# A graph layer and an expert layer on one core: who does the last blocks' work at the ends of the edge stages, and in which pieces the first dense batch runs

## The reference

```python
xn = layernorm(h, ln1);  q, k, v = xn@wq+bq, xn@wk+bk, xn@wv+bv       # per layer
scores = einsum('ehd,ehd->eh', q[dst], k[src]) / sqrt(32)            # edges and self loops
ex  = exp(scores - segment_max(scores, dst)[dst])
agg = segment_sum(ex/segment_sum(ex, dst)[dst] * v[src], dst)        # where deg > 0
h = h + agg@wo + bo
h = h + gelu(layernorm(h, ln2)@w1 + b1)@w2 + b2
...
x = x + h
out = x + layernorm(xf + sum of the two chosen experts' FFN(xf)),  xf = layernorm(x)
```

## Time and profile before

| what | value |
|---|---|
| median of 3 runs | 3311.08 us (3309.96 to 3312.67) |
| the profiled execution's own time | 3308.49 us |
| its span, first to last instruction | 3306.30 us |
| mean granted TensorE clock | 0.772 of full speed |
| busy: PE / DVE / ACT / POOL | 68% / 75% / 40% / 55% |
| DMA | 623.51 MB, mean 189 GB/s |

### The profile page before, as it was taken

One profiled execution on the slowest core, in us unless ns is written; L12 is line 12 of the kernel. 1 busy time (PEld: TensorE's weight loads), 2 busy tenths in 40 slices (PEclk: granted clock), 3 DMA queues, 4 the chain that ended last, 5 costly groups with the idle time before them and its releaser, 6 DMA issues. The chain is left out here.

```text
span 3306.3 us, 28610 instructions
## 1 busy us (share of the span) xinstructions
PE 2235.3 (68%) x7207; PEld 1510.9 (46%) x7207; DVE 2490.4 (75%) x3966; ACT 1320.9 (40%) x3886; POOL 1834.8 (55%) x1938
## 2 busy tenths in 40 slices
PE   6745666656566666699956665666666666699798
PEld 4423443433343343476643333344433433477676
DVE  6788888888888888545448888888888888455233
ACT  2224444445545444211224444554544544222222
POOL 5047777777777776212047777777777775221000
PEclk8866767677777766799976777777677767699899
DMA  5357777777777778323357777777777777332111
GB/s 145 105 169 236 243 243 243 243 243 243 245 246 246 243 243 244 84 62 86 82 162 236 244 243 243 243 245 245 246 246 243 244 243 234 78 79 55 45 32 39
DMA packets 249750, 623.51 MB, mean 189 GB/s; under 512 B 50258, under 2 KB 105777, under 8 KB 249592
## 3 DMA queue, kind: packets, MB, share of 16 engines
q0 software_dynamic: 149904, 471.38, 47.9%
q1 hardware_dynamic: 99688, 150.30, 14.6%
HBM read 526.66 MB, written 94.78 MB: 188 GB/s over the span
## 5 line engine op out<-in xcount | busy, mean ns | idle before, releaser
L811 POOL DMA_INDIRECT ring<-kv_table,stage_ix x1760 | 1672.7, 950 | 601.6 <-issue 539.7
L1078 PE MATMUL bank<-ring,hot_w 128*128 128x272 f32 x1760 | 709.9, 543 | 516.9 <-DVE ring L2026 467.3
L1065 PE MATMUL bank<-qs,hot_q 128*128 x1760 | 691.5, 535 | 358.4 <-DVE ring L2003 295.6
L1078 PEld LDWEIGHTS bank<-ring,hot_w 128*128 128x128 f32 x1760 | 418.1, 259 | 790.9 <-DVE ring L2026 630.6
L2003 DVE TENSOR_TENSOR ring<-ring,bank 128x1024 f32<-128x1024 f32 x440 | 533.7, 1213 | 282.0 <-DMA ring<-kv_table,stage_ix 254.9
L1065 PEld LDWEIGHTS bank<-qs,hot_q 128*128 128x128 f32 x1760 | 444.6, 263 | 513.0 <-issue 423.9
L2008 DVE TENSOR_REDUCE s<-ring 128x32 f32<-128x1024 f32 x440 | 533.9, 1213 | 4.2
L1293 ACT ACTIVATE hot_q<-pos_b,row_of 128x128 f32<-128x128 bf16 x880 | 301.0, 392 | 25.2 <-DVEq L1991 16.5
L2020 DVE TENSOR_TENSOR bank<-ring,bank 128x512 f32<-128x512 f32 x440 | 301.8, 686 | 0.0
L2017 DVE TENSOR_TENSOR ring<-ring,bank 128x512 f32<-128x512 f32 x440 | 297.7, 677 | 0.0
L2026 DVE TENSOR_TENSOR ring<-ring,bank 128x512 f32<-128x512 f32 x440 | 295.9, 673 | 0.4
(11 more groups left out here) (333 smaller groups left out, 2214.8 us busy)
## 6 DMA issues: line engine op xcount, KB each, us to landing
agg_d<-stage_o SPq DMA_DIRECT2D x108, 544.0 KB, 4.4
ring<-kv_table,stage_ix POOLq DMA_INDIRECT x1760, 3.8
pos_b<-rel_d SPq DMA_DIRECT2D x54, 256.0 KB, 5.4
kv_table<-ring SPq DMA_DIRECT2D x50, 224.0 KB
h_dram<-ring SPq DMA_DIRECT2D x15, 560.0 KB
ring<-h_dram SPq DMA_DIRECT2D x15, 560.0 KB
ring<-in_x_dram SPq DMA_DIRECT2D x10, 560.0 KB
ring<-kv_table SPq DMA_DIRECT2D x10, 560.0 KB
```

The source lines that it names most:

```text
L811: gps.indirect_dma_start(out=chunk[:, par * G + i, j, :], out_offset=None, in_=table, in_offset=bass.IndirectOffsetOnAxis(ap=stage_ix[:, p ...
L1065: mm = ten.matmul(q_bank(third, i)[:, 0:QC], hot_q[:, i % 4, a * P:(a + 1) * P], qs[:, bass.ds(t * QC + a * QC, QC)], start=(a == 0), stop ...
L1078: mm = ten.matmul(b_acc[i % 2][:, lo - OWN:MC], hot_w[:, i % 4, :], chunk[:, s, j, lo:ROW], start=(j == 0), stop=(j == QD // 2 - 1), skip_ ...
```

## The change

It has six parts.

1. For the last blocks of each layer, `weigh_late` multiplies all four rows of a block in one VectorE instruction, and the second pair of rows is added to the first by GpSimd (`add_pairs`), behind all its gathers. These are blocks 2 to 7 of the last full group and all four of the last group. VectorE's order in the last two steps is written anew: in the last full group two late multiplications stand ahead of the last score product.
2. SP waits until the last block's gathers have landed before it issues the weight loads.
3. PE's `fold` is cut into `fold_rows` and `fold_ups`. The row part for mid, and the up part for last, are issued inside the links, ahead of the sums over first rows; the up part for mid stays behind the links.
4. The first batch's home gathers count a semaphore per tile (`first0` to `first4`), and VectorE's `first_head` works tile by tile: denominators, own term and division of a tile, mixed with the addition of the projected tile and statistics of earlier ones. The bias is added at the start.
5. PE projects tile j - 1 of that batch right behind the transposes of tile j.
6. `hold` becomes a plain wait wherever its counter was read by nobody.

```diff
+LATE = 2
+assert LASTG == LATE + 2 and LATE + 3 == G - 3
+HEAD0 = 5 * BT + 1
...
                     if nn == LASTG:
+                        sp.wait_ge(gath[(NB - 1) % SLOTS], (layer + 1) * uses((NB - 1) % SLOTS) * QD * 16)
                         next_weights()
                     if nn:
...
-                                               in_offset=bass.IndirectOffsetOnAxis(ap=stage_h[:, j:j + 1], axis=0)).then_inc(s["home"], 16)
+                                               in_offset=bass.IndirectOffsetOnAxis(ap=stage_h[:, j:j + 1], axis=0)).then_inc(s["home"] if it else S[f"first{j}"], 16)
...
-                            hold(pool, S["agg"], (k - 2) * G + (layer * NB + i + 1), S["pool_passed"])
+                            pool.wait_ge(S["agg"], (k - 2) * G + (layer * NB + i + 1))
...
+                def add_pairs(par, i, n):
+
+                    pool.wait_ge(S["weighed"], n + 1)
+                    val = chunk[:, par * G + i, :, D:ROW]
+                    gps.tensor_tensor(val[:, 0:2], val[:, 0:2], val[:, 2:4], ALU.add).then_inc(S["w_ready"], 1)
+
                 for k in range(NGRP):
                     group(k, k % 2, blocks_of(k), k < 2)
+                for k in range(NGRP - 2, NGRP):
+                    for i in range(LATE if k == NGRP - 2 else 0, blocks_of(k)):
+                        add_pairs(k % 2, i, layer * NB + k * G + i)
 
...
-            def fold(kind):
+            def fold_rows(kind):
 
                 pe.wait_ge(S["w_in_dma"], 16 * W_TOTAL[kind])
-                mm = None
                 if kind in ("in", "mid"):
                     for c0, c1, b in ((0, 512, bank[7 if kind == "in" else 4]), (512, 768, bank[2 if kind == "in" else 5])):
                         for a in range(2):
                             mm = ten.matmul(b[0:TN, 0:c1 - c0], g_col[:, 1, a:a + 1].to_broadcast([P, TN]), w_qkv[:, a, c0:c1], start=(a == 0), stop=(a == 1))
-                if kind in ("mid", "last"):
-                    for f in range(FFN // P):
-                        for a in range(2):
-                            mm = ten.matmul(bank[6][:, f:f + 1], w_up[:, a, f * P:(f + 1) * P], g_col[:, 3, a:a + 1], start=(a == 0), stop=(a == 1))
+                    mm.then_inc(S["w_pe"], 1)
+
+            def fold_ups(kind):
+
+                pe.wait_ge(S["w_in_dma"], 16 * W_TOTAL[kind])
+                for f in range(FFN // P):
+                    for a in range(2):
+                        mm = ten.matmul(bank[6][:, f:f + 1], w_up[:, a, f * P:(f + 1) * P], g_col[:, 3, a:a + 1], start=(a == 0), stop=(a == 1))
                 mm.then_inc(S["w_pe"], 1)
 
...
-                turn(0)
-                project(0, 0)
+                for j in range(BT + 1):
+                    if j < BT:
+                        turn_tile(0, j)
+                    if j:
+                        project_tile(0, 0, j - 1)
...
                 mm.then_inc(S["l_pe"], 1)
+                if layer:
+                    fold_ups("last")
+                else:
+                    fold_rows("mid")
                 pe.wait_ge(S["l_dve"], layer * L_DVE + L_FIRST)
                 for a in range(2):
...
             links(0)
-            fold("mid")
+            fold_ups("mid")
             pe.wait_ge(S["w_dve"], 2)
...
             links(1)
-            fold("last")
             pe.wait_ge(S["w_dve"], 3)
             staggered("last")
...
-                v.wait_ge(S["w_pe"], PASS_NO[kind] + 1)
+                v.wait_ge(S["w_pe"], {"in": 1, "mid": 2, "last": 4}[kind])
...
                 if kind in ("mid", "last"):
+                    v.wait_ge(S["w_pe"], {"mid": 3, "last": 4}[kind])
                     ws.did(tt(up_bias[:, :], up_bias[:, :], bank[6][:, 0:FFN // P], ALU.add))
                     for a in range(2):
...
+                def first_head(h, st):
+
+                    hd = Steps(s["head"])
+                    v.wait_ge(s["x_in"], 2 * ROWS)
+                    hd.did(bias(h_n[kind], bias_sq))
+                    v.wait_ge(s["out_free"], 1)
+
+                    def put(j):
+                        v.wait_ge(s["mm"], j + 1)
+                        tt(h[:, j, :], h_n[kind][:, j, :], bank[4 + j % 3][0:TN, 0:D], ALU.add).then_inc(s["bank_free"], 1)
+
+                    def stats(j):
+                        v.wait_ge(s["bank_free"], j + 4)
+                        st.did(vec.bn_stats(stat[:, j, :], h[:, j, :]))
+
+                    for j in range(BT):
+                        v.wait_ge(S[f"first{j}"], (1 if kind == "mid" else 2) * 16)
+                        own, z = home[:, j, 0:H], home[:, j, H:2 * H]
+                        val = home[:, j, 2 * H:MC].rearrange("p (d h) -> p d h", h=H)
+                        den = small[0:TN, j * H:(j + 1) * H]
+                        mine = own_v[:, j, :].rearrange("p (d h) -> p d h", h=H)
+                        hd.did(tt(den, z, own, ALU.add))
+                        hd.did(tt(mine, mine, own.rearrange("p (a h) -> p a h", a=1).to_broadcast([TN, DH, H]), ALU.mult)); hd.sync(v)
+                        hd.did(ts(den, den, 1e-30, None, ALU.max))
+                        hd.did(tt(mine, mine, val, ALU.add)); hd.sync(v)
+                        hd.did(vec.reciprocal(den, den)); hd.sync(v)
+                        tt(tok[:, j, :].rearrange("p (h d) -> p d h", h=H), mine, den.rearrange("p (a h) -> p a h", a=1).to_broadcast([TN, DH, H]), ALU.mult).then_inc(s["tok"], 1)
+                        if j >= 2:
+                            put(j - 2)
+                            if j >= 3:
+                                stats(j - 3)
+                    assert hd.n == HEAD0, hd.n
+                    put(BT - 2)
+                    stats(BT - 3)
+                    put(BT - 1)
+                    stats(BT - 2)
+                    stats(BT - 1)
+                    st.sync(v)
+                    aggregate()
+
...
-                head(0)
                 st = Steps(s["dve"])
-                projected(0, 0, 0, h_of[0], st)
+                first_head(h_of[0], st)
                 rooted(0)
...
+                def weigh_late(par, i, n):
+
+                    val = chunk[:, par * G + i, :, D:ROW].rearrange("p j (d h) -> p j d h", h=H)
+                    w = w_of[:, i].rearrange("p j (a h) -> p j a h", a=1)
+                    tt(val, val, w.to_broadcast([P, QD, DH, H]), ALU.mult).then_inc(S["weighed"], 1)
+
...
                     ch.did(vec.tensor_reduce(top[:, 0:nk * H].rearrange("p (b h) -> p b h", h=H), s, AX.X, ALU.max))
-                    if not first:
+                    if not nn:
+                        weigh_late(1 - par, G - 3, n - 3)
+                    elif not first:
                         weigh(1 - par, G - 3, n - 3)
                     ch.sync(v)
                     ch.did(tt(s[:, :, :, QD], s[:, :, :, QD], pen[:, :, QD:QD + 1].to_broadcast([P, nk, H]), ALU.add))
-                    if not first:
+                    if not nn:
+                        weigh_late(1 - par, G - 2, n - 2)
+                    elif not first:
                         halve(1 - par, G - 3, n - 3)
                         weigh(1 - par, G - 2, n - 2)
                     v.wait_ge(S["lanes"], (k + g0) * 2 + 1)
@@ -2048,11 +2126,13 @@
                     ch.did(vec.tensor_tensor_scan(f_lane[lanes, :], pen_now[lanes, 0:P], b_ch[lanes, 0:P], -BIG, ALU.add, ALU.max))
                     ch.sync(v)
                     ch.did(vec.tensor_tensor_scan(m_lane[lanes, ::-1], pen_now[lanes, 1:P + 1][:, ::-1], f_lane[lanes, ::-1], -BIG, ALU.add, ALU.max))
-                    if not first:
+                    if nn and not first:
                         halve(1 - par, G - 2, n - 2)
                     if nn:
                         scores(1 - par, 0, tn, n + nk, third + 1)
-                    if not first:
+                    if not nn:
+                        weigh_late(1 - par, G - 1, n - 1)
+                    elif not first:
                         weigh(1 - par, G - 1, n - 1)
                     if nn:
                         sum_scores(1 - par, 0, n + nk)
@@ -2060,15 +2140,38 @@
                     m = b_ch[:, P:P + nk * H].rearrange("p (b h a) -> p b h a", h=H, a=1).to_broadcast([P, nk, H, QD + 1])
                     ch.did(tt(s, s, m, ALU.subtract))
                     assert ch.n == CHAIN
-                    if not first:
+                    if nn and not first:
                         halve(1 - par, G - 1, n - 1)
+
+                    def sum_weights():
+                        v.wait_ge(S["weights"], (k + g0) * 2 + 2)
+                        vec.tensor_reduce(chunk[:, par * G:par * G + nk, 0, WOFF:D], w_of[:, 0:nk].rearrange("p b j h -> p b h j"), AX.X, ALU.add).then_inc(S["z_sum"], 1)
+
+                    if nn == LASTG:
+                        for i in range(LATE):
+                            scores(1 - par, i + 1, tn, n + (nk + i + 1), third + 1)
+                            if i == 0:
+                                sum_weights()
```

(17 more changed lines are left out.)

78 lines of the change are left out of this document (41 added, 37 removed).

## The result

The changed kernel takes 3283.59 us (median of 4 runs, 3282.53 to 3283.89) beside 3311.07 us for the kernel before on the same chip (4 runs, 3309.96 to 3312.67). The ratio is 0.9917, 95% interval 0.9902 to 0.9933: 27.5 us faster, where 13.4 was forecast. The profiled execution after took 3283.58 us (span 3281.6), 24.9 less than the profiled one before; the other 2.6 us are the distance of that one from its median.

The account below looks back on a forecast made before the run. GpSimd's gathers, about 1.25 us each, were taken to bound the long middle, so only both layers' ends could move. 5.2 + 2.7 + 0 - 2.3 + 4.0 + 3.8 = 13.4 us, from 3311.08 to 3297.7; range 3292 to 3302.

Parts of the forecast that it names:

- the wait for the last gather in layer 1: Layer 1's edge end: VectorE was taken to start without waiting for a gather, so nothing to win; layer 0's wait was 3.40 us.
- the markers: Semaphore increments behind waits, before GpSimd's gathers and VectorE's statistics: removing them was put at nothing.
- VectorE's share of the row pairs: Late blocks of both edge stages: 0.68 us less VectorE time per block, ten blocks, 6.8 us per layer.
- the tiles of the first batch: First dense batch: 16.3 us from first home landing to aggregation, gaining 4.0 us in layer 0 and 3.8 in layer 1.
- Row pairs to GpSimd: Both edge ends: VectorE's saving less waits and tail ends layer 1's evacuations 2.7 us earlier, and likewise layer 0's.
- T: Time of one GpSimd addition of 128x512 in the edge ends: taken as 1.34 us, between 0.67 and 2.5.
- the waits: Last group: VectorE's scans and the subtraction wait behind PE's queue, 1.0 and 0.8 us given back, 1.8 per layer.
- The tail: End of each edge stage: last block passes through GpSimd before PE, costing T + 0.6 us, taken as 1.9.
- Weight loads: Layer 0's edge end: loads behind the last gather remove the 3.40 us wait, less 0.9 for a late put; layer 1 nothing.
- Folds inside the links: Links: layer 0's row fold put at 0, bounds +0.3 and -0.9; layer 1's up fold a loss of 2.3 us.
- Layer 1's -2.3: Layer 1's links: up fold of 6.83 us in a gap of 4.58 delays the link chain 2.3 us; bounds 0 and -2.3.
- everything at its good end: Rival, both ends: T = 0.67, links +0.3 and 0, tiles 5.3 and 5.1; 22.2 us gained, 3289; chance 0.10.

## Why the prediction was wrong in size

Two terms that were put at nothing failed outright: the wait for the last gather in layer 1, and the markers. Two were right in mechanism and too small: VectorE's share of the row pairs, and the tiles of the first batch.

**Row pairs to GpSimd.** The mechanism was right, and T nearly so: 1.27 us for 1.34. The Trainium skill (GPSIMD Engine Reference, 4.1 Engine selection) has GpSimd about twice as slow on such an addition; the trace agrees, 1.27 against VectorE's 0.69, and the move pays all the same, since GpSimd had nothing else to do. What failed is the size of VectorE's share. In layer 0, from 1310.86 to the end of its last instruction of the stage, VectorE needed 23.1 us before (to 1337.34, less the wait of 3.40) and 17.2 after (1310.84 to 1328.07): 5.9 saved where 6.8 - 1.8 = 5.0 was forecast. A late block costs 1.13 us from start to start. Six of the ten blocks took 1.92 before, since their halving starts 0.03 us behind the end of its multiplication where I had 0.08 ahead of it: 0.79 saved, not 0.68. The other four, with an instruction of the chain or of the scores in between, save 0.67. That is 7.4 for 6.8; the waits were 0.66 us, with 0.87 for the longer scan, not 1.8. The tail cost 1.63 us (GpSimd's last addition ends at 1329.70), not 1.94. With the 3.40 us wait gone that is 5.9 - 1.63 + 3.40 = 7.7, beside the 7.6 measured. In layer 1 the same terms without the wait give 4.2 of the 5.2 us, and the rest is the different start named under the table.

**"Layer 1 has no such wait, nothing to win"** failed outright. It was read from one execution, without asking when its loads were issued. Other executions with the old edge stage have that wait in layer 1, 2.81 and 4.48 us, and their edge end of layer 1 takes 32.15 and 33.87 us, not 30.52. With the late multiplications ahead of the last product it is 24.2 to 25.9 in every run with delayed loads. The median gains 2.6 us more than the two profiled executions show; such a wait in most executions of the kernel before would account for it, which is not shown, as only three traces with the old edge stage exist.

**Weight loads.** The mechanism was right: moved back alone, the loads brought waits for the last gather of 0.80 and 2.23 us, and no trace with delayed loads has one. Alone the delay is worth 0 to 2.2 us a layer, since the late multiplications cover most of the wait; the put was not late (0 lost, 0.9 forecast), as SP needed 12.4 us for the loads (1311.10 to 1323.51), not 16.8.

**Folds inside the links.** Layer 0 was taken as an either-or, and both happened: the row fold ran 5.43 us at the low clock, so that the sums started 0.9 us later, and then these took 2.00 us instead of 3.97. The links are 0.9 shorter by it, beyond the bound of +0.3, and it brings nothing to the end (the run with the row fold back is as fast). Layer 1's -2.3 came out as -2.2 by luck: against the run with the fold moved back that stage is 3.1 us longer (16.60 and 13.52), and without the fold in it, it was 0.9 shorter than before. Not foreseen were 0.8 us more in the next stage, where the delayed scatter ran beside VectorE's scaling and bias.

**First batch by tiles.** From the first landing to the aggregation it took 14.1 us in layer 0 (1354.33 to 1368.42) and 14.2 in layer 1, not 16.3: a tile costs VectorE 1.75 us from start to start (1354.33 to 1356.08), not the 2.05 of its durations added up, and less remained behind the last tile. The prediction allowed for the overlap with the late multiplications and forgot it here. The first home landed 5.3 and 4.4 us after its issue, later than 4.28.

**"Markers removed. Nothing"** is the second step that failed outright: 4.3 us alone (1.3 to 7.6 by the interval). The rows it rested on the earlier trace rows were not places where an instruction waits for the one just before it.

Added up over the runs that take one part each: pairs 11.1, markers 4.3, tiles 8.2 and about 4 more in layer 0 once the folds are over sooner (23.23 to 19.38), loads about 2 (not clear of the spread), the up fold -4.9: some 25 us, beside 27.5 and 24.0 (3307.43 less 3283.47) in two measurements. The runs stand on several chips, so the sum is rough. Of the rivals, none came; "everything at its good end" was the nearest, with other terms than its own: T was not 0.67, and the up fold did not fit.

## What to carry to other kernels

An end of a stage that waits for a transfer has to be read in several executions, and beside the times at which other transfers are issued: one trace showed the wait in one layer and not in the other, and the change removed it in both. A price for a small thing, such as a semaphore increment, is taken where the instruction behind it is waited for, not where it is one of a thousand in a queue with slack. And before an instruction is moved into an idle stretch, look at when each of its operands lands, and at which engine shares its way to memory there.

## What the runs showed of the hardware

GpSimd and VectorE hold each other up. VectorE's scan of 32x128 with both operands in SBUF took 1.28 us beside GpSimd's additions, two of which end at 1320.97, 0.28 us ahead of it, and 0.41 with one operand in PSUM beside the same additions. In the other direction, GpSimd's gather of home rows took 2.21 us beside VectorE's addition of 125x1280, and 1.24 without it; it ended 1.1 us after that addition did (1350.13 and 1351.25). The Trainium skill (SBUF — State Buffer, Who interferes with whom) has it that a VectorE instruction with two SBUF inputs contends with a GpSimd instruction that reads SBUF; the trace agrees for the scan, and for the gather in so far as it reads its row numbers from a tile in SBUF (`stage_h`). The same section of the Trainium skill tells of a probe in which a VectorE operation on two tensors, unlike a copy, did not stall a DMA; here the instruction that issues the indirect gather is held, and the measurement decides. A home gather of the next batch that had begun 0.64 us ahead of such an addition took 1.48 us (1371.65 and 1372.29 in the kernel after).

TensorE's eight sums of 110x272 took 3.97 us at a granted clock of 0.50 and 2.00 at 1.00. With eight wide products ahead of them (5.43 us of the row fold in layer 0; 5.05 us, put there for that alone, in layer 1) the clock was 1.00; with the up fold's 32 narrow ones ahead, 6.99 us at 0.50, it stayed at 0.50, in the kernel after and in three more runs with the fold there. Wide products are not the only work it rose behind: in the run with the row fold back it was 0.50 during the eight sums and 0.96 right behind them.
